# Second cross attention: attention outputs by four pairs of heads, 512 columns a product

## The reference, cut to what matters

```
x = x + _L1_xattn_ref(_layernorm(x, axis=-1), ctx_1024, ctx_1024, L1_xattn_w_q, L1_xattn_w_k, L1_xattn_w_v, L1_xattn_w_o)

def _L1_xattn_ref(query, key, value, w_q, w_k, w_v, w_o):
    scale = HEAD_DIM ** (-0.5)                     # 16 heads of 64
    q = (query @ w_q).reshape(B, Q, HEADS, HEAD_DIM).transpose(0, 2, 1, 3)
    k = (key @ w_k).reshape(B, Kl, HEADS, HEAD_DIM).transpose(0, 2, 1, 3)
    v = (value @ w_v).reshape(B, Kl, HEADS, HEAD_DIM).transpose(0, 2, 1, 3)
    scores = jnp.einsum('bhqd,bhkd->bhqk', q, k) * scale
    attn = jax.nn.softmax(scores, axis=-1)
    out = jnp.einsum('bhqk,bhkd->bhqd', attn, v)
    out = out.transpose(0, 2, 1, 3).reshape(B, Q, HEADS * HEAD_DIM)
    return out @ w_o
```

## Time and profile before

| | |
|---|---|
| three runs | 952.36, 955.69, 958.51 us |
| profiled execution | 957.4 us, of which span 955.7 us |
| busy over the span | PE 909.0 us (95%), DVE 630.7 (66%), ACT 500.7 (52%), POOL 197.2 (21%) |
| granted TensorE clock, mean | 0.983 |
| second cross attention | about 377 to 810 us of the span |

### The profile page before, as it was taken

One profiled execution on the slowest core, in us unless ns is written; L12 is line 12 of the kernel. 1 busy time (PEld: TensorE's weight loads), 2 busy tenths in 40 slices (PEclk: granted clock), 3 DMA queues, 4 the chain that ended last, 5 costly groups with the idle time before them and its releaser, 6 DMA issues. The chain is left out here.

```text
span 955.7 us, 20196 instructions
## 1 busy us (share of the span) xinstructions
PE 909.0 (95%) x8260; PEld 745.7 (78%) x8260; DVE 630.7 (66%) x866; ACT 500.7 (52%) x721; POOL 197.2 (21%) x190
## 2 busy tenths in 40 slices
PE   8999999887989998989999999999999999998996
PEld 7888888755669997569898999999988877567554
DVE  5667776668734345599797989798979752376222
ACT  5777777544466663665554565646464541312331
POOL 2000000020214441422221331404050210421101
...
GB/s 162 78 63 50 49 50 5 3 67 0 70 46 80 95 88 58 163 132 229 245 196 235 218 245 222 219 239 223 236 223 255 211 233 4 276 337 260 342 337 115
DMA packets 103848, 151.92 MB, mean 159 GB/s; under 512 B 11009, under 2 KB 84434, under 8 KB 103762
## 3 DMA queue, kind: packets, MB, share of 16 engines
...
## 5 line engine op out<-in xcount | busy, mean ns | idle before, releaser
L189 PE MATMUL ps<-f_pT_hi,f_cN_hi 128*128 128x256 f32 x512 | 146.4, 286 | 5.4 <-DVE f_pT_lo L1898 5.3
L189 PE MATMUL ps<-f_pT_lo,f_cN_hi 128*128 128x256 f32 x512 | 147.7, 288 | 0.0
L189 PE MATMUL ps<-f_pT_hi,f_cN_lo 128*128 128x256 f32 x512 | 146.0, 285 | 0.0
L448 DVE SCALAR_TENSOR_TENSOR a_u<-ps,a_floor,a_cap 128x1024 f32<-128x1024 f32 x64 | 79.2, 1279 | 48.2 <-PE ps L543 47.8
L189 PEld LDWEIGHTS ps<-f_pT_hi,f_cN_hi 128*128 128x128 f32 x512 | 97.1, 190 | 9.7 <-DVE f_pT_lo L1898 7.9
L1749 POOL TENSOR_TENSOR f_cN_lo<-e_raw,f_cN_hi 128x512 fp32r<-128x512 f32 x32 | 49.7, 1578 | 262.0 <-ACT f_cN_hi L1776 262.0
L189 PEld LDWEIGHTS ps<-f_pT_hi,f_cN_lo 128*128 128x128 f32 x512 | 98.8, 193 | 0.0
L189 PEld LDWEIGHTS ps<-f_pT_lo,f_cN_hi 128*128 128x128 f32 x512 | 97.2, 190 | 1.0
L1898 DVE TENSOR_TENSOR f_pT_lo<-f_pT_lo,f_pT_hi 128x1024 fp32r<-128x1024 f32 x64 | 81.4, 1297 | 23.9 <-ACT f_pT_hi L1785 23.9
L359 ACT ACTIVATE a_pr<-a_u,a_nb 128x1024 f32<-128x1024 f32 x64 | 73.8, 1153 | 43.7 <-DVE a_u L448 42.5
L1785 ACT CAST f_pT_hi<-f_pT_lo 128x1024 fp32r<-128x1024 f32 x64 | 66.8, 1049 | 55.0 <-DMA f_pT_lo<-f_turned_rows 54.9
...
## 6 DMA issues: line engine op xcount, KB each, us to landing
f_turned_rows<-f_turned SPq DMA_DIRECT2D x64, 512.0 KB, 4.5
f_pT_lo<-f_turned_rows SPq DMA_DIRECT2D x256, 128.0 KB, 3.3
k_w<-in_L_ffn_W SPq DMA_DIRECT2D x30, 1024.0 KB, 14.8
a_ctxT<-in_ctxT SPq DMA_DIRECT2D x16, 512.0 KB, 4.5
...
e_raw<-in_ctxT SPq DMA_DIRECT2D x8, 1024.0 KB, 8.0
...
```

The source lines that it names most:

```text
L189: last = nc.tensor.matmul(out, a[i], b[j], start=start and n == 0, stop=stop and n == 2, skip_group_check=skip)
L448: V.scalar_tensor_tensor(u[:, n % NU, :].rearrange("p (r w) -> p r w", r=RT), core.psum[:, 0:2048].rearrange("p (r w) -> p r w", r=RT)[:, ...
```

## The change

Outputs are made for four pairs at a time, a *round* R (0 to 15): 512 columns a product, half as many products. O(R) fills bank 6 (first half of the features) and bank 7 (second half). TensorE makes four pairs of scores, 4R + 5 to 4R + 8, then O(R). In the texts A to D are those four pairs, in this order; pairs 4R to 4R + 3 feed O(R), the last of them the C of the round before. Probabilities lie in a ring of three doubles (two pairs each) instead of two groups; where a round's doubles stand in the ring in the other order, its pairs' columns are exchanged (`columns`). There are three score buffers, banks 0 to 5. The split queries are kept for two doubles instead of a batch. `e_raw` has half its size and holds features or keys by turns, in `contexts(R)`: features of a later batch in even rounds, keys of the next in odd ones. The split of w_o moves from the tail to round 12.

```diff
-        both = core.sb("e_raw", [P, DC * S + KT * D], F32, ctx)
-        rawT = both[:, 0:DC * S].rearrange("p (c s) -> p c s", s=S)
-        raw = both[:, DC * S:DC * S + KT * D].rearrange("p (k d) -> p k d", d=D)
+        raw = core.sb("e_raw", [P, KT * D], F32, ctx)
+        rawT = raw[:].rearrange("p (c s) -> p c s", s=S)
...
-        NPR = 2
+        NPR, NSC = 2, 3
...
-        qb = [core.sb("e_qb_" + n, [P, DC, H * T], F32R, ctx) for n in ("hi", "lo")]
+        qb = [core.sb("e_qb_" + n, [P, 2, DC, 2 * P], F32R, ctx) for n in ("hi", "lo")]
...
+        def act_queries(act, d):
+            if d >= 2:
+                act.wait_ge(s_psum, 2 * d - 2)
+            nc.scalar.copy(qb[0][:, d % 2, :, :], queries_of(d)).then_inc(qb_hi, 1)
...
+            if n % 2 == 0:
+                pe.wait_ge(qb_lo, d + 1)
+            wait_if_positive(pe, exp_ready, n + 1 - NSC)
...
+                    last = product3(nc, core.ps[n % NSC][:, 512 * k:512 * k + 512],
+                                    [q[:, d % 2, c, P * (n % 2):P * (n % 2) + P] for q in qb],
...
+        def columns(n):
+            return n % HP ^ 2 if n // HALF % 3 == 2 else n % HP
...
+            pT_hi = sb("pT_hi", [P, 3, 8, KM * QD], F32R)
+            pT_lo = sb("pT_lo", [P, 3, 8, KM * QD], F32R)
...
+            o2 = [t[:].rearrange("p c s -> p (c s)").rearrange("p (r n) -> p r n", n=NT) for t in cT[1]]
...
+            def double(n):
+                return (n // 2 + 1) % 3
+            def moved(tile, n):
+                return tile[:, double(n), 4 * (n % 2):4 * (n % 2) + 4, :]
+            def key_rows(tile, R, m):
+                first, second = sorted((double(HALF * R), double(HALF * R + 2)))
+                return tile[:, first:second + 1:second - first, :, QD * m:QD * m + QD]
...
+                    R = n // HALF
...
+                    free = R - 2 if n % HALF < 2 else R - 1
+                    if free >= 0:
+                        sp.wait_ge(o_psum, 2 * free + 2)
...
+                def contexts(R):
+                    b = R // 2
+                    if R % 2 == 0 and b < B - 1:
                         sp.wait_ge(n_hi, 2 * b + 2)
                         sp.wait_ge(n_lo, 4 * b + 4)
...
                         if b + 2 < B:
                             load_features(sp, b + 2)
                         else:
-                            sp.dma_start(wv, a["L1_xattn_w_v"].rearrange("(c p) o -> p c o", p=P)).then_inc(v_in, 16)
+                            sp.dma_start(wo, a["L1_xattn_w_o"].rearrange("(h p) o -> p h o", p=P)).then_inc(wo_in, 16)
+                    elif R % 2 == 1:
+                        if b + 2 < B:
+                            sp.wait_ge(t_hi, 2 * b + 6)
+                            sp.wait_ge(t_lo, 4 * b + 12)
+                        else:
+                            sp.wait_ge(wo_hi, 1)
+                            sp.wait_ge(wo_lo, 1)
+                        load_keys(sp, b + 1)
+                    else:
+                        sp.wait_ge(n_hi, 2 * B)
+                        sp.wait_ge(n_lo, 4 * B)
+                        sp.dma_start(wv, a["L1_xattn_w_v"].rearrange("(c p) o -> p c o", p=P)).then_inc(v_in, 16)
+                sp.wait_ge(t_hi, 2)
+                sp.wait_ge(t_lo, 4)
+                load_features(sp, 1)
+                sp.wait_ge(t_hi, 4)
+                sp.wait_ge(t_lo, 8)
+                load_keys(sp, 0)
+                put(0)
+                put(1)
+                fetch(0)
+                fetch(1)
+                put(2)
+                put(3)
+                put(4)
+                for R in range(NR - 1):
+                    n = HALF * R + HALF
+                    fetch(n - 2)
+                    fetch(n - 1)
+                    fetch(n)
+                    contexts(R)
+                    put(n + 1)
+                    put(n + 2)
+                    fetch(n + 1)
+                    put(n + 3)
+                    if n + 4 < PAIRS:
+                        put(n + 4)
+                fetch(PAIRS - 2)
+                fetch(PAIRS - 1)
...
+                pool_features(pool, 1)
                 for b in range(B):
-                    if b >= 1:
-                        keys(b, 0)
-                        keys(b, 1)
-                    if b + 1 < B:
-                        pool_features(pool, b + 1)
-                pool.wait_ge(wo_hi, 1)
-                nc.gpsimd.tensor_tensor(wo2[1], wo, wo2[0].bitcast(F32), ALU.subtract).then_inc(wo_lo, 1)
+                    keys(b, 0)
+                    keys(b, 1)
+                    if b + 2 < B:
+                        pool_features(pool, b + 2)
+                    elif b + 2 == B:
+                        pool.wait_ge(wo_hi, 1)
+                        nc.gpsimd.tensor_tensor(wo2[1], wo, wo2[0].bitcast(F32), ALU.subtract).then_inc(wo_lo, 1)
...
+                def queries(d):
+                    if d < NG:
+                        act.wait_ge(c_act, 4 * d + 4)
+                        act.wait_ge(c_dve, 4 * d + 4)
+                    act_queries(act, d)
...
-                first_queries(1)
-                first_queries(2)
+                queries(1)
+                features(1, 0)
                 evict(6)
                 exponentials(1)
                 evict(7)
-                first_queries(3)
-                act.wait_ge(c_psum, UNITS)
+                queries(2)
+                features(1, 1)
+                exponentials(2)
+                high(0)
+                exponentials(3)
+                queries(3)
+                high(1)
+                exponentials(4)
                 keys(0, 0)
                 keys(0, 1)
-                for b, g in groups[1:]:
-                    G = NG * b + g
-                    if G >= 3:
-                        outputs(G - 3)
-                    if g == 2:
-                        if b >= 1:
-                            keys(b, 1)
-                        if b + 1 < B:
-                            features(b + 1, 0)
-                            features(b + 1, 1)
-                    if g == 3 and b + 1 < B:
-                        queries(b + 1, 0)
-                    if g == 0:
-                        queries(b, 1)
-                    exponentials(2 * G)
-                    exponentials(2 * G + 1)
-                    high(2 * G - 2)
-                    if g == 1 and b >= 1:
+                for R in range(NR - 1):
+                    n, d, b = HALF * R + HALF, 2 * R + 4, (R + 1) // 2
+                    if R >= 1:
+                        outputs(R - 1, 1)
+                    if R % 2 == 0 and R >= 1:
+                        keys(b, 1)
+                    if n + 4 < PAIRS:
+                        queries(d)
+                    exponentials(n + 1)
+                    high(n - 2)
+                    high(n - 1)
+                    exponentials(n + 2)
+                    if n + 4 < PAIRS:
+                        queries(d + 1)
+                    high(n)
+                    exponentials(n + 3)
+                    if n + 4 < PAIRS:
+                        exponentials(n + 4)
+                    if R % 2 == 0 and b + 2 < B:
+                        features(b + 2, 0)
+                        features(b + 2, 1)
+                    if R % 2 == 0 and b + 2 == B:
+                        act.wait_ge(wo_in, 16)
+                        act.wait_ge(s_psum, HP * (B - 1))
+                        nc.scalar.copy(wo2[0], wo).then_inc(wo_hi, 1)
+                    outputs(R, 0)
+                    if R % 2 == 1:
                         keys(b, 0)
-                    high(2 * G - 1)
-                outputs(LAST - 2)
-                act.wait_ge(wo_in, 16)
-                nc.scalar.copy(wo2[0], wo).then_inc(wo_hi, 1)
+                    high(n + 1)
...
...
+                dve_queries(dve, 2)
+                maximum(2)
+                maximum(3)
+                divide(2)
+                turn(2)
+                dve_queries(dve, 3)
+                low(0)
+                divide(3)
+                turn(3)
+                maximum(4)
+                low(1)
+                divide(4)
+                turn(4)
+                for R in range(NR - 1):
+                    n, d = HALF * R + HALF, 2 * R + 4
+                    maximum(n + 1)
+                    if n + 4 < PAIRS:
+                        dve_queries(dve, d)
+                    divide(n + 1)
+                    maximum(n + 2)
+                    low(n - 2)
+                    low(n - 1)
+                    turn(n + 1)
+                    maximum(n + 3)
+                    divide(n + 2)
+                    turn(n + 2)
+                    if n + 4 < PAIRS:
+                        dve_queries(dve, d + 1)
+                    low(n)
+                    if n + 4 < PAIRS:
+                        maximum(n + 4)
+                    divide(n + 3)
+                    turn(n + 3)
+                    if n + 4 < PAIRS:
+                        divide(n + 4)
+                        turn(n + 4)
```

(44 more changed lines are left out.)

200 lines of the change are left out of this document (62 added, 138 removed).

## The result

The changed kernel takes **977.28 us** (median of 4 runs, 976.65 to 979.15), the kernel before 957.1 beside it (4 runs, 952.36 to 959.4): a ratio of 1.0221, 95% interval 1.0177 to 1.0264. Slower by 20 us, where +9.3 was forecast; inside the range, at its upper end. The profiled execution took 977.18 us, its span 975.5.

A forecast was written before the change was run, and what follows sets the result against it. The prediction took TensorE, busy without a hole, to bound the kernel. Its terms -10.1 + 17.5 - 5.7 + 6.5 + 0.5 + 0.5 = +9.2 us, put on the median 955.69, gave 965 us, range 954 to 978.

The forecast's parts named there:

- Start: Before O(0): put(0) leaves 12.7 us late, O(0) near 456 instead of 430.15, TensorE idles 20.4 us; +17.5 us.
- The rounds: Steady rounds: TensorE (22.0 us) and the turned probabilities' road (22.1) meet; 0.45 us extra a round, 14 rounds, +6.5 us.
- Circle (b): Rounds: loop from low(C) through VectorE's turns, put(C), put(D), fetches and high back to low(C); 22.1 us.
- The cause named: Rounds: a 1 MB load just ahead of put(A) may keep fetch(A) running when put(C) leaves; 0 to 1.2 us a round.
- Width: Output products: 768 of 512 columns at 229.2 ns replace 1536 of 256 at 121.2 ns; -10.1 us.
- the 235: Output products: the prediction called itself wrong if they come over 235 ns apart.
- Rival 4: Output products: 512 strided columns cost close to 2 x 121 ns, so the wide product saves little; 973 us, chance 0.04.
- rival 2: Rounds: load, fetch(A) and put(C) queue up, so the road binds, 1.2 to 1.6 us over 22.0; 978 us, chance 0.18.
- Clock: Start's gaps or a round: the clock falling once costs some 1.7 us; +0.5 us taken.
- Tail: Last round: low(59) needs 10.0 us against 8.25 of scores ahead of O(14); +0.5 us, between 0 and 3.
- Old stalls: Rounds: the 5.7 us of TensorE stalls in the kernel before go away with the old order; -5.7 us.

The follow-up runs named there:

- e2: The changed kernel with put(0), put(1), fetch(0) and fetch(1) issued ahead of the waits for features(1)'s split and the first key load: 970.6 us, ratio 1.0112.
- e3: The changed kernel with SP's put of pair D behind the fetches of B and C, at the start put(4) behind fetch(2) and fetch(3): 967.43 us, ratio 1.0082.
- e8: The changed kernel with the rounds' loads cut to 32 of 1024 feature columns and one of eight key blocks, waits and splits kept: 977.45 us, ratio 1.0175.
- e6: The changed kernel with POOL splitting only 32 of each 512 columns of the next features in the rounds: 971.33 us, ratio 1.013.
- e1: The changed kernel with the 512 columns an output product reads in one run instead of 16 runs of 32: 975.88 us, ratio 1.0148.

## Why the prediction was wrong, point by point

- **Start (+17.5): right.** put(0) at 422.69 (423), O(0) at 455.53 (456): 25.4 us later with three pairs of scores (8.25) more done, +17.1. e2 and e3 show its two parts, the load ahead of put(0) and put(4) ahead of fetch(2) and fetch(3). Of the 20.4 us of idling forecast some 5 were slow work instead, 24.29 us for 84 products at a mean granted clock of 0.79; O(0) wasn't later for that, since TensorE still waited 5.02 us for a low ahead of it.
- **The rounds (+6.5): the step that failed.** A round was put at 22.45 us (22.0 and 0.45) and took 22.87, which is 14 x 0.42 = 5.9 of the 10.6 us that the forecast lacks. Circle (b) came out at 22.1 because it took every divide and low at its undisturbed length, and its way from turn(C) to high(C) at 9.8 us. Measured are 11.8 in odd rounds and 10.55 in even ones: POOL's split makes divide(D) 1.1 us longer, and both fetches stand behind the put(D) that waits for it. SP's order was in the step, the slow divide was not, and even the undisturbed 10.55 is over the 9.8 taken. That makes the odd rounds' road 22.9 to 23.6, the mean over rounds 22.9. The price read off the rounds is near the forecast, 12 x 0.5 = 6.0 from O(1) to O(13), but by luck, as TensorE needed 22.36 and not 22.0. The cause named, the load beside fetch(A) and put(C), was wrong: e8 takes it away and nothing changes, e6 takes POOL away and the stalls go. (14 x 0.45 is 6.3, not 6.5, so the sum as worked out is 9.0.)
- **Width (-10.1): mis-sized.** 768 x (2 x 121.2 - 236.7) = -4.4 us, and 236.7 is over the 235 that the prediction named as a sign of being wrong. The scores' 229 didn't carry over, since their operand is one run. But the 6 us lacking here are not what the result lacks: e1 gives products of 227 ns, and the rounds stay at 22.9. With the width as forecast, the rounds would have cost 6 us more than forecast. Rival 4 had the pitch half right, rival 2 the road as the bound, from another cause and at 22.9 rather than 23.4.
- **Clock (+0.5): too small.** O(0) ran 2 us long. In e2, with 7 us less of idling, it took 13.8 us at a granted clock of 0.81, in e3 11.7 at 0.98; what decides it stays open.
- **Tail (+0.5): too small.** O(14) waited 2.34 us, inside the bounds given, and then ran 1.7 us long at the lower clock; e2 and e6 waited as long there (2.56 and 2.43 us) and kept the full clock. O(15) waited 0.34. Of the waits of 1 to 1.5 in the old tail the trace before shows one of 0.67, at 791.19. Some +3.7.
- **Old stalls (-5.7): as costed.**

Sum: -4.4 + 17.1 + 2.0 - 5.7 + 6.0 + 3.7 = +18.7, against 975.5 - 955.7 = 19.8 of the span. The 1.1 left over are not assigned.

The slow divide could have been read ahead of the change. In the trace before, beside POOL's split of features:

```profile
574.44 1.53 DVE L1613 TENSOR_SCALAR xnT<-xnT,e_total 128x1024 f32<-128x1024 f32 x1
...
571.17 5.96 POOL L1595 TENSOR_TENSOR e_cT_lo<-e_raw,e_cT_hi 128x512 fp32r<-128x512 f32 x4
```

TensorE was busy for all of 550 to 600 us there, so that divide cost nothing before the change.
